# Switch layer of a vision tower: results stored by plain transfers and gathered back, rows turned by identity products, constant products on TensorE during routing

## The reference

```python
x_flat = x.reshape(-1, d)                     # 2056 x 256, after a layer norm
logits = x_flat @ router_w.T + router_b       # 32 experts
routed_idx = jnp.argmax(logits, axis=-1)
def expert_mlp(w1, b1, w2, b2):               # 256 -> 64 -> 256
    h = jax.nn.relu(x_flat @ w1 + b1)
    return jax.nn.relu(h @ w2 + b2)
y_all = jax.vmap(expert_mlp)(weights1, bias1, weights2, bias2)
out_flat = y_all[routed_idx, jnp.arange(n)]   # then added to the residual h
```

## Time and profile before

| | |
|---|---|
| median of 3 runs | 4349.88 us (4332.42 to 4360.74) |
| the profiled execution | 4347.72 us |
| its span, first to last instruction | 4345.6 us |
| mean granted TensorE clock over the span | 0.933 of 2.4 GHz |
| TensorE matmul busy | 3598.7 us (83%) |
| switch layer | from about 4119 us to the end |

### The profile page before, as it was taken

The page is one execution under the profiler, slowest core; times in us unless marked ns, Lnnn a source line. Parts: engine busy times, 40 slices in busy tenths (PEclk is TensorE's granted clock), DMA queues, the critical chain, the costliest instruction groups (busy, mean ns, idle before and its releaser), DMA issues. The chain is left out here.

```text
span 4345.6 us, 61242 instructions
## 1 busy us (share of the span) xinstructions
PE 3598.7 (83%) x19616; PEld 2465.4 (57%) x19616; DVE 2666.3 (61%) x3928; ACT 2071.4 (48%) x4736; POOL 1925.0 (44%) x1894
## 2 busy tenths in 40 slices
PE   2868878898888788888888888888887788888867
PEld 1545475565654456666666666666655555555544
DVE  6432124444222699999999999999994333333331
ACT  1321112223111677777777777777762243334321
POOL 0122200000022499898999999898982000000034
PEclk9889969999999799999999999999999999999965
DMA  3057620000176100000000000000000000000035
GB/s 89 2 207 270 227 73 1 1 1 28 59 257 230 33 1 1 2 1 2 1 13 1 3 1 1 2 1 2 1 1 10 25 1 1 1 1 1 3 106 152
DMA packets 66640, 196.96 MB, mean 45 GB/s; under 512 B 12704, under 2 KB 37401, under 8 KB 55993
## 3 DMA queue, kind: packets, MB, share of 16 engines
q1 hardware_dynamic: 54968, 161.81, 11.2%
q0 software_dynamic: 11328, 30.95, 2.3%
HBM read 166.74 MB, written 25.99 MB: 44 GB/s over the span
## 5 line engine op out<-in xcount | busy, mean ns | idle before, releaser
L1876 DVE TENSOR_TENSOR_SCAN ssm_hs<-ssm_da,ssm_pb 128x512 f32<-128x512 f32 x1024 | 1240.4, 1211 | 3.6 <-ACT ssm_da L1715 3.6
L1415 POOL TENSOR_TENSOR ssm_hc<-ssm_hs,ssm_cb 128x1024 f32<-128x1024 f32 x512 | 1207.3, 2358 | 0.0
L1512 PE MATMUL ssm_py<-ssm_hc,ident 128*128 128x256 f32 x4096 | 1059.1, 381 | 3.7 <-POOL ssm_hc L1415 3.7
L1715 ACT ACTIVATE ssm_da<-ssm_dt,ssm_an 128x255 f32<-128x255 f32 x2048 | 871.5, 502 | 132.0 <-POOL ssm_dtu L1363 88.4
L1512 PEld LDWEIGHTS ssm_py<-ssm_hc,ident 128*128 128x128 f32 x4096 | 704.6, 191 | 79.0 <-POOL ssm_hc L1415 5.4
L1859 DVE TENSOR_TENSOR ssm_pb<-ssm_pb,ssm_dtu 128x512 f32<-128x512 f32 x1024 | 694.2, 678 | 26.2 <-PE ssm_pb L1498 24.0
L1498 PE MATMUL ssm_pb<-ssm_bst,ssm_eyeb 96*128 96x256 bf16 x2048 | 403.5, 279 | 210.5 <-DVE ssm_hs L1876 195.2
L1498 PEld LDWEIGHTS ssm_pb<-ssm_bst,ssm_eyeb 96*128 96x128 bf16 x2048 | 147.2, 98 | 488.0 <-DVE ssm_hs L1876 413.8
L1114 DVE TENSOR_REDUCE duo_mxr<-duo_ring 128x4 f32<-128x1024 f32 x128 | 156.6, 1224 | 315.9 <-PE duo_ring L847 304.9
L2343 PE MATMUL moe_pu<-moe_up,moe_xt 128*128 128x512 f32 x568 | 275.0, 607 | 59.7 <-issue 57.6
L2215 POOL DMA_INDIRECT moe_xr<-moe_x_dram,moe_rowx x71 | 68.7, 967 | 428.7 <-PE ln_ps L2332 267.0
(11 more groups left out here) (590 smaller groups left out, 6069.7 us busy)
## 6 DMA issues: line engine op xcount, KB each, us to landing
moe_up<-in_moe_up SPq DMA_DIRECT2D x72, 1024.0 KB, 5.4
moe_down<-in_moe_down SPq DMA_DIRECT2D x72, 512.0 KB, 6.2
sw_wt<-in_sw_w SPq DMA_DIRECT2D x47, 192.5 KB
moe_x_dram<-moe_tok SPq DMA_DIRECT2D x32, 128.0 KB
moe_yg<-moe_y_dram SPq DMA_DIRECT2D x16, 256.0 KB
tok_w<-in_wd SPq DMA_DIRECT2D x4, 576.0 KB, 13.0
out<-h SPq DMA_DIRECT2D x1, 2056.0 KB, 7.4
tok_pix<-in_img SPq DMA_DIRECT2D x1, 2048.0 KB, 9.7
```

Source lines behind the costliest of these rows:

```text
L1415: nc.gpsimd.tensor_tensor(hc[:, n % 2, part_], hs[:, n % 2, part_], cb[:, q * NQ_ + 4 * half:q * NQ_ + 4 * half + 4, :], ALU.mult).then_in ...
L1512: ins = nc.tensor.matmul(py[:, j % 2, 0:L], k.ident[:], hc[:, n % 2, st, :], start=False, stop=(q == QN - 1 and st == NQ_ - 1))
L1715: ins = nc.scalar.activation(da[:, n % 2, 2 * m + o, 1:L], dt2[:, v, j, 1:L], ACT.Exp, scale=a_n[:, d, j, st:st + 1])
L1876: nc.vector.tensor_tensor_scan(two(hs[:, n % 2, 2 * m:2 * m + 2, :]), two(da[:, n % 2, 2 * m:2 * m + 2, :]), two(pb[:, p % 4]), 0.0, ALU.m ...
```

## The change

For the switch layer alone (`not glu`):

- After each result ScalarE itself stores the block's 128 rows of `yo` to rows `b * 128` and on of `y_dram`, a plain DMA on its own queue, after waiting for its own copy. GpSimd's scatters are gone, and so are the three VectorE operations for their row numbers.
- `row_y` now holds for each token the slot of its result (`slot_f`). After the last gather of the loop GpSimd waits for all stores and gathers the 17 chunks of results by it, with indirect DMAs, into `yg`. SyncE's 17 plain loads are gone.
- The rows of a block, and the chunks on the way back, are turned by a product with the identity instead of a transpose (two passes instead of one).
- TensorE makes products of the identity with 512 columns of `k.x` that nobody reads (`keep_going`): 5 after the last router copy, 14 after the ranking products, 4 after `invert`.
- The signals `gsem` belong to the whole program instead of the layer.

```diff
@@ gpsimd
                 for b in range(NBLK + behind):
                     if b < NBLK:
                         fetch(b)
-                    if b >= behind:
+                    if b >= behind and glu:
                         send(b - behind)
+                if not glu:
+                    pool.wait_ge(s["row_y_set"], 1)
+                    for v in range(YR):
+                        pool.wait_ge(ysem[v], 16 * len(range(v, NBLK, YR)))
+                    for m in range(NCK):
+                        w = chunk_width(m)
+                        if m >= GR:
+                            pool.wait_ge(s["mixed"], m - GR + 1)
+                        nc.gpsimd.indirect_dma_start(yg[0:w, m % GR, 0, :], None, y_dram, bass.IndirectOffsetOnAxis(ap=row_y[0:w, m:m + 1], axis=0)).then_inc(gsem[m % GR], 16)
@@ tensor
+                def keep_going(n):
+
+                    for r in range(n):
+                        nc.tensor.matmul(pl[:, 0, 0:512], k.ident[:], xf[:, r % 2, 0:512], start=True, stop=True)
+
+                if not glu:
+                    pe.wait_ge(s["tok_out"], NCK)
+                    keep_going(5)
                 pe.wait_ge(s["hot_in"], 1)
...
+                    keep_going(0 if glu else 14)
                     invert()
+                    keep_going(0 if glu else 4)
...
-                        ins = nc.tensor.transpose(px(b)[:, c * P:c * P + P], xr[:, b % XR, c * P:c * P + P], k.ident[:])
+                        dst, src = px(b)[:, c * P:c * P + P], xr[:, b % XR, c * P:c * P + P]
+                        ins = nc.tensor.transpose(dst, src, k.ident[:]) if glu else nc.tensor.matmul(dst, src, k.ident[:], start=True, stop=True)
...
-                            ins = nc.tensor.transpose(dst, y[:, 0, :], k.ident[0:w, 0:w])
+                            ins = nc.tensor.matmul(dst, y[:, 0, :], k.ident[0:w, 0:w], start=True, stop=True)
@@ scalar
                     nc.scalar.activation(yo[:, b % YR, :], pl[:, 1, 0:D], ACT.Copy if glu else ACT.Relu).then_inc(s["y_in"], 1)
+                    if not glu:
+                        act.wait_ge(s["y_in"], b + 1)
+                        act.dma_start(y_dram[b * P:b * P + P], yo[:, b % YR, :]).then_inc(ysem[b % YR], 16)
@@ vector
+                    else:
+                        nc.vector.tensor_copy(row_y[:], slot_f[:, 0, :]).then_inc(s["row_y_set"], 1)
```

More of the change, by code:

```diff
@@ L2093, in section_sparse @@
         inv, row = sb("inv", [P, 3, NBLK]), sb("row", [P, 2, NBLK])
-        row_x, row_y = sb("rowx", [P, NBLK], U32), sb("rowy", [P, NBLK], U32)
+        row_x, row_y = sb("rowx", [P, NBLK], U32), sb("rowy", [P, NBLK if glu else NCK], U32)
         gdiag = sb("gdiag", [P, K, NCK, P]) if K == 2 else None
@@ L2124, in section_sparse @@
         x_dram = nc.dram_tensor(tag + "_x_dram", [NTOK, D], F32).ap()
-        y_dram = nc.dram_tensor(tag + "_y_dram", [K * ROWS + NBLK * P, D], F32).ap()
-        y_back = y_dram[0:K * ROWS].rearrange("(j r) d -> r j d", j=K)
+        y_dram = nc.dram_tensor(tag + "_y_dram", [(K * ROWS if glu else 0) + NBLK * P, D], F32).ap()
+        y_back = y_dram[0:K * ROWS].rearrange("(j r) d -> r j d", j=K) if glu else None
         names = ("r_in s_in x_out pid_set onehot inverted row_x_set row_y_set gdiag_set rw_set mean cent sqd var log std free xn_set skipped turned tok_out hot_in ranked gate_in exp_in gate_set "
@@ L2133, in section_sparse @@
         ysem = [signal(nc, k.ctx, tag + "_y_out%d" % v) for v in range(YR)]
-        gsem = [signal(nc, k.sems, tag + "_g_in%d" % v) for v in range(GR)]
+        gsem = [signal(nc, k.sems if glu else k.ctx, tag + "_g_in%d" % v) for v in range(GR)]
         sq = [k.ln_sq, k.ln_cen]
@@ L2196, in _ @@
                     sp.wait_ge(ysem[v], 16 * len(range(v, NBLK, YR)))
-                for m in range(NCK):
+                for m in range(NCK if glu else 0):
                     w = chunk_width(m)
@@ L2649, in take_rows_of_slots @@
                     nc.vector.tensor_copy(row_x[:], row[:, K - 1, :]).then_inc(s["row_x_set"], 1)
-                    link(nc.vector.tensor_tensor(inv[:, 0, :], inv[:, 0, :], spare[:], ALU.mult))
-                    link(nc.vector.tensor_tensor(inv[:, 0, :], spare[:], inv[:, 0, :], ALU.subtract))
-                    link(nc.vector.tensor_tensor(row[:, 0, :], row[:, 0, :], inv[:, 0, :], ALU.add))
-                    nc.vector.tensor_copy(row_y[:], row[:, 0, :]).then_inc(s["row_y_set"], 1)
+                    if glu:
+                        link(nc.vector.tensor_tensor(inv[:, 0, :], inv[:, 0, :], spare[:], ALU.mult))
+                        link(nc.vector.tensor_tensor(inv[:, 0, :], spare[:], inv[:, 0, :], ALU.subtract))
+                        link(nc.vector.tensor_tensor(row[:, 0, :], row[:, 0, :], inv[:, 0, :], ALU.add))
+                        nc.vector.tensor_copy(row_y[:], row[:, 0, :]).then_inc(s["row_y_set"], 1)
+                    else:
+                        nc.vector.tensor_copy(row_y[:], slot_f[:, 0, :]).then_inc(s["row_y_set"], 1)
                 if shared:
@@ L2707, in _ @@
                     dve.wait_ge(s["free"], B + ahead)
-        close_section(k, [*s.values(), *wsem, *gsem])
+        close_section(k, [*s.values(), *wsem, *(gsem if glu else ())])
 def build(nc, a, out, last):
```

## The result

| first series, one chip | before | after |
|---|---|---|
| median of 18 runs each | 4348.71 us (4331.55 to 4368.13) | 4368.86 us (4352.97 to 4385.71) |
| ratio after / before | | 1.0051, 95% interval 1.0034 to 1.0069 |
| span of the profiled execution | 4345.6 us | 4364.9 us |
| first turn to the end of the last result copy ("the loop") | 138.9 us | 144.7 us |
| from there to the end of the last addition ("the way back") | 15.8 us | 30.2 us |

The change made the kernel 0.5% slower on this chip, where 4333 us, 17 us under before, had been forecast; 4368.86 lies inside the range, on the side of the rival "clock lost at the first pause and not regained". The two stretches of the last layer add up to 5.8 + 14.4 = 20.2 us, and the medians differ by 20.15.

What follows compares the result with a forecast made beforehand. TensorE was taken to pace the last layer's loop at half clock, 2.52 us a block. Costs +31.1, fast blocks -42.0 and pauses -5.7 gave -16.6 us on 4347.7, 4331; adjusted to the median, 4333 us, range 4306 to 4382.

Steps and rivals of the forecast that it cites:

- clock lost at the first pause and not regained: Rival for the block loop: some 5 fast blocks, +25 us, 4375 us; wholly slow up to 4387; chance 0.32.
- Does the clock hold?: Deciding question for the block loop: total change 31.1 - 1.20 n us for n fast blocks, breaking even at 26.
- n = 35: Block loop: three quarters of the 46 pitches at the fast clock, 31.1 - 42.0 = -10.9 us.
- lost at some of the pauses, regained in between: Forecast for the loop's clock, high on entry: -16.6 us with fewer pauses, 4333 us; chance 0.38 including the transfer case.
- a third of its passes: Argument against the lost-clock rival: a third of the old loop's passes were transposes or ran at half height.
- three signs of a wrong mechanism: Clock high but blocks over 2.1 us apart; loop at 0.50 from its first block; way back growing under 8 us.
- The second rule: Loop's clock return: transposes don't count as busy, so identity products let it return; otherwise they only cost 0.43 or 0.22 us a block.
- with time: Loop pauses, 19.7 us in 136, were taken as proportional to time; a shorter loop gives back 5.7 us.
- Way back +10.8: After the loop: 17 gathers 1.27 us apart instead of 0.63 us chunks, and later landing, add 10.8 us.
- Fast block 1.75: Loop pitch at the fast clock, from the larger of 1.69 us (TensorE) and 1.72 us (transfers).
- the rival with 2.05 us: Transfers bound the fast loop at 2.05 us a block: -15 us with n = 46; chance counted within the forecast's 0.38.
- Constants 0.5: Unread products while routing and before the loop: cost 0 to 2.3 us, taken as 0.5.

Runs made afterwards that it cites:

- A: Chip of the first series, kernel before against the changed kernel: 4348.71 and 4368.86 us, ratio 1.0051.
- E: Chip of a later series: changed kernel a third time 0.9975 of before, the same with a 128-row second product 0.9945.
- B: Chip of the series that took the change apart: no constants 1.0017, plain transfers alone 1.0034, scatters kept 1.0033, 128-row second product 0.9993 of before.
- D: Chip of a later series, perhaps the first series' chip again: before took 4348.99 us; changed kernel with different rows gathered for empty slots 1.0054 of before.
- full height, transposes, spread: Changed kernel with 128-row second-layer product, transposes for the loop's turns, and different rows gathered for empty slots: 0.9896 of before, loop 80.0 us.
- transfers only: Kernel before with ScalarE's plain stores and GpSimd's gathers on the way back; transposes kept, no constants: 1.0034 of before, loop 121.2 us.
- C: Chip of a later series: before again 0.9994 with loop 119.0 us, changed kernel again 0.9994 with loop 101.7 us.
- spread rows: Changed kernel with empty slots gathering 128 different rows instead of all row 0: 1.0054 of before on one chip, 0.9916 on another.
- the two kernels meant to part these: Changed kernel with GpSimd three gathers ahead instead of six, 0.9985 of before; changed kernel with eight weight buffers instead of six, 0.9976.
- F: Chip of the last series: changed kernel with different rows for empty slots 0.9916 of before; with 128-row product, transposes and ten result buffers too, 0.9907.

## Why the prediction was wrong

**Failed: "Does the clock hold?", n = 35, "lost at some of the pauses, regained in between".** On A the clock was lost at the first pause and not regained, n = 4, and 31.1 - 1.20 x 4 = +26.3 us is within 6 us of the 20.2 found. That nearness is in part luck: by the same sum the loop would be 15.0 us longer and the way back 10.8, and they were 5.8 and 14.4. "Regained in between" was wrong for the changed kernel on all three chips that ran it: the slow loop "2.56 of 2.95 us columns, none of them transposes" did not bring it back. I had named the half-height products as an argument against holding and not carried it into the return. One edit, 128 rows instead of 65, turned that around: on E 1.00 was back after 6.9 us instead of not at all in 40.6. (The rival's "a third of its passes" was wrong as well: two of eight were transposes and two ran over 65 rows, and those two stayed.) None of the three signs of a wrong mechanism that I had listed came, and a clock lost for good was not among them.

**The second rule did not decide the return, as I had let it.** With full height, transposes held 1.00 for the loop's first 55.4 us and came back to it after 6.8 us, so identity products were not what the return needed. The Trainium skill (TensorE: Matmul & The Clock Gate, Part 4) has it that transposes don't count as busy for the gate. Whether they count by themselves no run here shows, since in these loops six passes of eight were products and could have been enough. With 65 rows the turns did matter: without constants, on chip B, the loop with identity products was up after 6.4 us and the one with transposes never. At full height the identity products were a cost: 1.66 instead of 1.38 us a fast block, and the slow one is 3.05 instead of 2.52. Beside half-height products the changed loop had 55 to 65 fast microseconds on chips without the stop, and the transposed ones none or 10.

**The pauses: right that they matter, wrong that they come "with time".** There are two kinds. The stops with the releaser called remote are in all six profiles of A and D and in none of the fourteen of the other four chips; without scatters they did not recur in the loop after the first, at 3.05 us a block or at mostly 1.4 to 2 (full height, transposes, spread on D), while with scatters there were eight. So in the changed kernel on A seven of the eight went, with the scatters. An estimate of their worth is 138.9 - 121.2, the loop of before on A less that of transfers only on B: some 18 us, not the 5.7 forecast, which does not come out of its own rule either (19.7 us in 136, for a loop 22 us shorter, is 3.2). The other kind was in no trace of before: 15 empty blocks that gather one row, which only the fast loops waited for.

**On the other chips the forecast would have stood no better for its reason.** There the changed loop was fast for two thirds (n is 33 to 35 by the clock, where I took 35, but in one stretch and with no return: luck) and 13 to 17 us shorter than before's 119.0, the way back ate 10.5, and the time cannot be told from that of before (0.9994, 0.9975).

**Sizes.** Way back +10.8: measured +10.5 on chip C (and on E beside before on C), +14.4 on A. Slow block 2.95: 3.05. Fast block 1.75 for "transfers bound": 1.66, and 277 to 298 GB/s were sustained in the versions with transposes and spread rows, where I had taken 267 for the best (the changed kernel itself moved 255); the rival with 2.05 us is out. ScalarE's issue, 0.3 to 1.0: 0.33. Constants 0.5: first turn 2.95 us after the first gather's start, 2.98 before, so 0. The constants worked as told and bought 0.7 to 5.5 us of loop.

**Open.** What makes the stops of A and D: they came at SyncE's first weight issue in the loop and with GpSimd issuing back to back, but the two kernels meant to part these met a chip without them. That it is the chip rests on those six and fourteen, the kernel before, the changed one and the one with spread rows being in both groups. The 3.5 us more on the way back of A and D, in the four profiles with gathers there, sit in three to five chunks near one another, whose additions stand 2.1 to 3.5 us apart (2.80, 2.81, 2.82 on A) where C, E and F have 0.8 to 1.7 (B once 2.5); GpSimd issues gathers back to back there too, but whether it is the same stop was not tried.

## What to carry to other kernels

Before paying to hold the fast clock, ask what brings it back after one stall: a kernel that holds it only while nothing goes wrong took some 40 us more for its loop (144.7 against 101.7 and 105.9) on a chip where something does. Fill the array's height with zeros and ones already at hand before adding products. When a loop gets faster, look at what its padding does: rows that no one reads can be the dearest ones to fetch.

## What the runs showed of the hardware

- Gathers of one and the same 1 KB row from all partitions took 0.38 us a packet against 0.18 for 128 different rows, and raised every queue's landing from 4.9 to 9.9 us.
- With other work unchanged, TensorE's clock came back after 6.9 us with the second product over 128 rows, and not in the remaining 40.6 us of loop with it over 65 at 3.05 us a block (chip E; on A not in 134, although TensorE was busy in 100.00 of 100 us). It is no law of 65 rows: beside transposes, at 2.52 us a block, the clock rose once, after 44.9 us.
- A loop in which two of eight passes a block were float32 transposes of 128 columns held the clock at 1.00 for its first 55.4 us, as the one with products in their place did for 65.5.
- One and the same kernel fares differently from chip to chip: the changed kernel was at 1.0051 (1.0034 to 1.0069) on one, slower than before, and at 0.9994 and 0.9975 on two others, not told apart from it.
